# Attention and feed-forward in one block, the integer weights' size check inside attention's groups, Q and K low halves on VectorE

## The reference

```
ga, gb: size clamped to at least 0.25, sign kept
h = layernorm(x) * (1 + ca) + sa
q, k, v = split(h @ W_qkv + b_qkv)                 # 16 heads of 32
q = elu(q / sqrt(32)) + 1.0001 ; k = elu(k) + 1.0001
causal linear attention: kv += k v^T, ks += k, out = (q kv) / (q ks + 1e-6)
x = x + ga * (out @ W_out + b_out)
h = layernorm(x) * (1 + cb) + sb
x = x + gb * ((silu(h @ wg^T) * (h @ wu^T)) @ wd^T)  # wg, wu, wd: int32 / 127, hidden width 1536
```

## Time and profile before

| | us |
|---|---|
| median of 3 runs | 2226.02 (2223.32 to 2226.19) |
| profiled execution, its own time | 2222.91 |
| its span, first to last instruction | 2221.2 |
| TensorE matmul busy | 2144.6 |
| VectorE busy | 1242.6 |
| ScalarE busy | 829.9 |
| GpSimd busy | 846.0 |

### The profile page before, as it was taken

The page is one execution under the profiler, slowest core; times in us unless marked ns, Lnnn a source line. Parts: engine busy times, 40 slices in busy tenths (PEclk is TensorE's granted clock), DMA queues, the critical chain, the costliest instruction groups (busy, mean ns, idle before and its releaser), DMA issues. The chain is left out here.

```text
span 2221.2 us, 38713 instructions
## 1 busy us (share of the span) xinstructions
PE 2144.6 (97%) x15252; PEld 1748.3 (79%) x15252; DVE 1242.6 (56%) x1637; ACT 829.9 (37%) x1383; POOL 846.0 (38%) x634
## 2 busy tenths in 40 slices
PE   5999999999999999999779999999999999999999
PEld 3788887878888787888568888888888888888887
DVE  6988897888888788889732233322233322333211
ACT  4544444444444444444341233322233212332221
POOL 3644544443444444454323233332333323333333
PEclk9999999999999999999889999999999999999999
DMA  6111111111101111111531100111000111001100
GB/s 241 34 54 49 48 40 49 58 49 52 55 30 58 49 54 53 49 53 35 186 133 38 39 10 29 38 38 38 14 28 33 38 38 38 9 28 38 38 20 19
DMA packets 55319, 111.09 MB, mean 50 GB/s; under 512 B 4497, under 2 KB 4497, under 8 KB 55186
## 3 DMA queue, kind: packets, MB, share of 16 engines
q1 hardware_dynamic: 54658, 108.03, 13.9%
q10 hardware_dynamic: 528, 1.05, 0.1%
HBM read 75.50 MB, written 33.56 MB: 49 GB/s over the span
## 5 line engine op out<-in xcount | busy, mean ns | idle before, releaser
L1138 POOL TENSOR_TENSOR h_lo<-h,h_hi 128x512 fp32r<-128x512 f32 x192 | 248.1, 1292 | 498.0 <-ACT h_hi L1208 498.0
L1314 PE MATMUL dn<-wd,h_hi 128*128 128x512 f32 x768 | 298.8, 389 | 0.0
L1314 PE MATMUL dn<-wd,h_lo 128*128 128x512 f32 x768 | 298.8, 389 | 0.0
L1266 DVE TENSOR_TENSOR h<-gu,gate 128x512 f32<-128x512 f32 x192 | 132.4, 690 | 278.2 <-PE gu L1302 242.9
L1208 ACT ACTIVATE h_hi<-h 128x512 fp32r<-128x512 f32 x192 | 121.4, 632 | 386.1 <-DVE h L1266 386.1
L1205 ACT ACTIVATE gate<-gu 128x512 f32<-128x512 f32 x192 | 113.1, 589 | 373.8 <-PE gu L1302 373.8
L1302 PE MATMUL gu<-xt_hi,w_hi 128*128 128x512 f32 x768 | 213.1, 399 | 11.2 <-issue 11.2
L1279 DVE TENSOR_TENSOR fy<-dn,gb_row 128x512 f32<-128x512 f32 x64 | 44.2, 691 | 304.1 <-PE dn L1314 304.1
L656 DVE RECIPROCAL r_den<-r_den 128x512 f32<-128x512 f32 x64 | 213.7, 3339 | 0.0
L1302 PE MATMUL gu<-xt_hi,w_lo 128*128 128x512 f32 x768 | 208.1, 393 | 0.7 <-DVE h L1266 0.2
L1302 PE MATMUL gu<-xt_lo,w_hi 128*128 128x512 f32 x768 | 206.9, 391 | 0.0
(11 more groups left out here) (151 smaller groups left out, 3927.0 us busy)
## 6 DMA issues: line engine op xcount, KB each, us to landing
x_res<-in_L_attn_x SPq DMA_DIRECT2D x64, 256.0 KB, 2.7
x_mid<-x_res SPq DMA_DIRECT2D x64, 256.0 KB, 2.0
fx<-x_mid SPq DMA_DIRECT2D x16, 1024.0 KB, 5.6
out<-fy SPq DMA_DIRECT2D x64, 256.0 KB, 2.0
xg<-in_L_attn_x SPq DMA_DIRECT2D x15, 1024.0 KB, 5.5
fy<-in_L_ffn_w_down SPq DMA_DIRECT2D x12, 256.0 KB, 2.7
xg<-in_L_attn_x ACTq DMA_DIRECT2D x1, 1024.0 KB, 8.5
kt<-in_wmod_t SPq DMA_DIRECT2D x1, 1024.0 KB, 10.3
```

Source lines behind the costliest of these rows:

```text
L1138: pool.tensor_tensor(out=h_lo[:, j, :], in0=h[:, j % 2, :], in1=h_hi[:, j, :].bitcast(F32), op=ALU.subtract).then_inc(h_lo_ready, 1)
L1266: dve.tensor_tensor(out=h[:, j % 2, :], in0=gu[:, 2 * (j % 2) + 1, :], in1=gate[:, j % 2, :], op=ALU.mult).then_inc(h_ready, 1)
L1314: mm = pe.matmul(dn[:, t % 2, :], as_(half[:, j, t * P:(t + 1) * P]), as_(wd[:, j, :]), start=(j == 0 and half is h_hi), stop=(j == HB - 1 ...
```

## The change

There is one block. Each engine runs its attention program and goes on with its feed-forward program; there is no barrier. The feed-forward's tiles are attention's buffers, laid out so that the words land where their floats will stand and are converted in place. The weights come in one array ffn_words of 36 blocks of 128x512 words.

- The size check is spread over the loop's groups 2 to 13: three blocks each are loaded into a buffer `word`, reduced to their largest size, and merged. The comparison is in group 14. TensorE branches there, before the last part of group 14; its usual case is the Then, and holds the rest of attention and the whole feed-forward.
- The words are loaded once more, for conversion: gate and up columns 0 to 1023 in group 14, the rest and w_down in group 15. ScalarE converts them there.
- y shares a_t's buffer, so `divide` also waits for `residual` of the tile before.
- Q's and K's low halves are made by VectorE.
- In group 15 `k_turn` comes before `out_project`; the last tile's `k_turn`, `add_state` and `state_out` are gone. On GpSimd, prod_low of chunk 2 comes after the residual.
- The last out-projection, its gating and residual follow on hidden block 0 of the feed-forward. SyncE's load of groups 0 and 1 of x_mid and of gb come behind attention's last store.

The core of the diff (indentation of moved code is left out of account):

```diff
         @block.tensor
         def _(pe):
+            last_group, last_projection = attn.tensor(pe)
+            pe.wait_ge(att.wide_ready, 1)
+            flag = pe.value_load(wide[0:1, 0:1])
+            with pe.If(flag < 1):
+                last_group()
+                ffn.tensor(pe, True, last_projection)
+            with pe.Else():
+                last_group()
+                ffn.tensor(pe, False, last_projection)
...
-        y = sbuf(s, "y", [P, D])
+    y = a_t
...
+        def load_word(i):
+            wait(sp, most_ready, i + 1)
+            sp.dma_start(word[:, :].bitcast(I32), ffn_words[bass.ds(i, 1), :, :].rearrange("a p n -> (a p) n")).then_inc(word_in, 16)
...
             for t in range(GT):
                 tile = g * GT + t
                 load_residual(tile, t % 2, g * 2 + t // 2)
                 if not isinstance(tile, int) or tile > 0:
                     store(tile - 1, (t + 1) % 2)
+                if not isinstance(g, int) and t < 3:
+                    load_word(g * 3 + (t - 6))
+                if isinstance(g, int) and g == NG - 2 and t == 2:
+                    sp.wait_ge(pj_ready, (NG - 1) * UNITS + 2 * C)
+                    load_wide(words_hi, 0, 0)
+                    load_wide(words_lo, HB, 1)
+                if isinstance(g, int) and g == NG - 1 and t == 0:
+                    sp.wait_ge(pj_ready, NG * UNITS)
+                    load_rest(words_hi, 0, 2)
+                    load_rest(words_lo, HB, 3)
+                    sp.wait_ge(state_ready, (NG - 1) * GT)
+                    for j in range(HB):
+                        sp.dma_start(wd_words[:, j, :], ffn_words[2 * HB + j, :, :]).then_inc(words_in[4 + j // C], 16)
...
         def divide(tile, g, parity, t):
             wait(dve, num_ready, tile + 1)
             wait(dve, rden_ready, (g + 1) * C)
             wait(dve, a_lo_ready, tile)
+            wait(dve, y_ready, tile)
...
+        def word_size(i, slot):
+            wait(dve, word_in, i * 16 + 16)
+            dve.tensor_reduce(most[:, slot:slot + 1], word[:, :].bitcast(I32), AX.X, ALU.max,
+                              apply_absolute_value=True).then_inc(most_ready, 1)
+            wait(dve, most_ready, i + 2)
+            wait(dve, most_merged, i + 1)
+            dve.tensor_tensor(out=most_of_all[:, :], in0=most_of_all[:, :], in1=most[:, slot:slot + 1],
+                              op=ALU.max).then_inc(most_merged, 1)
...
-            for c in range(C):
-                xt_low(0, 0, c)
+        for k in range(C):
+            dve.wait_ge(qk_hi, k + 1)
+            dve.tensor_tensor(out=w_lo[:, k, 0:2 * D], in0=raw_qk[k // 2][:, k % 2, :],
+                              in1=w_hi[:, k, 0:2 * D].bitcast(F32), op=ALU.subtract).then_inc(qk_lo, 1)
+            xt_low(0, 0, k)
...
             divide(g * GT + 3, g, parity, 3)
+            if not isinstance(g, int):
+                word_size(g * 3 + (2 - 6), 2)
...
+        sp.wait_ge(att.a_ready, (NG - 1) * GT)
         load(0, 0)
+        sp.wait_ge(att.xt_ps, (NG + 1) * C)
+        load(1, 1)
+        sp.wait_ge(att.y_gated, NG * GT)
+        sp.dma_start(gb_row[:, :], gb_dram.broadcast_to([P, D])).then_inc(gb_in, 16)
...
                 dve.tensor_tensor(out=h[j % 2], in0=gu[2 * (j % 2) + 1], in1=gate[j % 2],
                                   op=ALU.mult).then_inc(h_ready, 1)
+                if isinstance(g, int) and g == 0 and j == 0:
+                    last_tile()
+                if isinstance(g, int) and g == 0 and j == 1:
+                    clamp_gb()
                 if ahead and j == 0:
                     norm_stats(g + 1, 1 - parity)
...
                     hidden(g, parity, j, wu, 2 * (j % 2) + 1, up_ps)
+                    if isinstance(g, int) and g == 0 and j == 0:
+                        last_projection()
```

More of the change, by code:

```diff
@@ L1 @@
+from collections import namedtuple
 from contextlib import ExitStack
@@ L101, in build @@
[L101 to L114 removed]
+        ga_row = sbuf(top, "ga_row", [P, D])
@@ new lines, in build, with _ @@
+        ffn = feed_forward(nc, top, sem, ident, mod_col, half_neg, w_hi, w_lo, xt_hi, xt_lo, norm, wide, gb_dram, ffn_words,
+                           att, shared, x_mid, out)
+        block = top.enter_context(nc.Block())
+        @block.sync
+        def _(sp):
+            attn.sync(sp)
+            ffn.sync(sp)
+        @block.gpsimd
+        def _(pool):
+            ffn.gpsimd(pool, attn.gpsimd(pool))
+        @block.scalar
+        def _(act):
+            attn.scalar(act)
+            ffn.scalar(act)
@@ new lines, in attention @@
+    z_exp = sbuf(s, "z_exp", [P, 2, GN])
+    z_relu = sbuf(s, "z_relu", [P, 2, GN])
+    kt, qt, v, r_den, probs, prod, prod_hi, prod_lo, k_sum, a_hi, a_lo = turned
+    words_hi, words_lo, wd_words = later.words_hi, later.words_lo, later.wd_words
+    xf = sbuf(s, "xf", [P, 2, GN])
+    k_past = sbuf(s, "k_past", [P, C])
+    kv_diag = sbuf(s, "kv_diag", [P, C, P])
+    k_tok = sbuf(s, "k_tok", [P, D])
+    a_t = sbuf(s, "a_t", [P, D])
+    x_res = sbuf(s, "x_res", [P, 2, D])
+    y = a_t
+    word = sbuf(s, "word", [P, D])
@@ new lines, in attention, with unit_of @@
+    raw_qk = [buf[:, :, :].rearrange("p c n -> p (c n)").rearrange("p (k n) -> p k n", k=2) for buf in (kt[1], qt[1])]
+    raw_v, raw_o = v[1], r_den[1]
+    wt_sa, wt_ca, wt_sb, wt_cb = kt[0], qt[0], v[0], r_den[0]
+    wm_late = (kt[1], qt[1])
+    late_bank = tuple(sc[:, i, :] for i in range(2))
+    c_bc = k_tok[:, :].rearrange("p (k n) -> p k n", k=C)
+    silu_row, junk = a_t, word
+    gb_row, ga_sign = a_t, word
+    def unit_of(u):
+        return (u % 2, u // 2) if u < 2 * C else (2, u - 2 * C)
@@ new lines, in vector, with tensor, x_turn, passes @@
+        groups(dve, 2, NG - 2, group)
+    def tensor(pe, exact, last_projection):
+        def x_turn(g, c):
+            wait(pe, xn_ready, g)
+            wait(pe, xf_ready, (g - 1) * C + c - 1)
+            for t in range(GT):
+                mm = pe.transpose(tp[c % 2][:, t * P:(t + 1) * P], xn[t][:, c * P:(c + 1) * P], ident[:, :])
+            mm.then_inc(xt_ps, 1)
+        def passes(exact):
+            return (lambda ap: ap) if exact else (lambda ap: ap.bitcast(F32))
+        def all_groups(exact):
+            as_ = passes(exact)
+            def hidden(g, parity, j, w, bank, done):
+                for i, (xt, k) in enumerate((xt, k) for xt in (xt_hi, xt_lo) for k in range(C)):
+                    mm = pe.matmul(gu[bank], as_(w[:, k, j * P:(j + 1) * P]), as_(xt[parity][:, k, :]),
+                                   start=(i == 0), stop=(i == 2 * C - 1))
+                mm.then_inc(done, 1)
+            def down(g, t):
+                wait(pe, y_gated, g * GT + t - 1)
+                for j in range(HB):
+                    if t == 0:
+                        wait(pe, h_lo_ready, g * HB + j + 1)
+                        if isinstance(g, int) and g == 0:
+                            pe.wait_ge(att.wd_ready, j + 1)
+                    for half in (h_hi, h_lo):
+                        mm = pe.matmul(dn[t % 2], as_(half[j][:, t * P:(t + 1) * P]), as_(wd[j]),
+                                       start=(j == 0 and half is h_hi), stop=(j == HB - 1 and half is h_lo))
+                mm.then_inc(dn_ps, 1)
+            def group(g, parity):
+                wait(pe, xt_lo_done, g * C)
+                if isinstance(g, int) and g == 0:
+                    pe.wait_ge(att.gu_ready, 4 * C)
+                    if not exact:
+                        pe.wait_ge(w_moved, 16 * 3 * HB)
@@ new lines, in group, with word_blocks @@
+                    if 4 <= j < 8 and (not isinstance(g, int) or g + 1 < NG):
+                        x_turn(g + 1, j - 4)
+                for t in range(GT):
+                    down(g, t)
+            groups(pe, 2, NG - 2, group)
+        all_groups(exact)
+    return Programs(sync, gpsimd, scalar, vector, tensor)
+_INS = ["L0_attn_x", "L0_attn_W_qkv", "L0_attn_b_qkv", "L0_attn_W_out", "L0_attn_b_out",
+        "L0_c", "L0_wmod"]
+_TURNED = ("L0_c",)
+def word_blocks(w_gate, w_up, w_down):
+    wide = [np.asarray(w).T.reshape(C, P, HID // D, D).transpose(0, 2, 1, 3).reshape(HB, P, D) for w in (w_gate, w_up)]
+    return np.concatenate(wide + [np.asarray(w_down).T.reshape(HB, P, D)])
```

2101 lines of the change are left out of this document (1012 added, 1089 removed).

## The result

The changed kernel takes 2216.64 us (median of 8 runs, 2214.95 to 2219.81), the kernel before 2224.53 us (8 runs) beside it: a ratio of 0.9966, 95% interval 0.9955 to 0.9977. It is faster by 7.9 us, where 13.8 were forecast.

What follows compares the result with a forecast made beforehand. TensorE was taken to bound the kernel, busy 2144.6 of 2221.2 us, leaving some 77 us. The terms -4.0 + 4.2 + 2.0 + 0.5 - 25.1 + 8.6 = -13.8 us gave 2212 us, range 2200 to 2222.

Steps and rivals of the forecast that it cites:

- Start, -4.0 forecast: Start: Q and K low halves on VectorE end the first projection near 32.8 instead of 36.8 us, 4.0 us gained.
- Loop, +4.2 forecast: Groups 2 to 13: checks and the later division cost 0.35 us a group behind the last check, 4.2 us lost.
- what is late in tiles 0 to 2 is caught up there: Loop, tile 3: VectorE, idle about 10 us a group, makes up the division's delay of 0.7 to 1.8 us.
- Branch, +2.0 forecast: Group 14: TensorE's branch on the size check, moved from the seam, costs 2.0 us.
- the bound from below: Branch in group 14: nearest from below was a loop's jump back, 4.7 us in 5.
- Conversions, +0.5: Groups 14 and 15: ScalarE's word copies stand ahead of the denominators and may make them late; 0.5 us lost.
- Last group, -25.1 forecast: Last group and seam: no reductions, earlier K turn, x rows' wait; feed-forward's second block at 1111.2, not 1136.38; 25.1 us gained.
- Feed-forward, +8.6 forecast: Feed-forward group 0: group 1's rows load late, TensorE waits 6 us, then half clock 2.6 us; 8.6 us lost.
- (a): Feed-forward: rows of group 1 arrive in time or VectorE is not held; no 8.6 us loss, 2203.6 us; chance 0.17.
- (b): Loop: VectorE-bound at tile 3's V rows, 2.1 us in 12 groups, 25.2 lost instead of 4.2; 2233 us; chance 0.08.
- (c): Last group keeps its pace (4 us), xt_lo always loses (4.2 us): 2220.4 us, no measurable change; chance 0.1.
- (d): Branch costs what it did at the seam, 4.6 us more: 2217 us; chance 0.15.

Runs made afterwards that it cites:

- the two runs: On the changed kernel: twelve unused VectorE reductions put back in the last group, 2223.46 us; last output projection ahead of the first hidden block, 2223.86 us.
- the other arm: The changed kernel with TensorE's condition turned round, so the usual weights take the arm that is jumped to; 2220.19 us, ratio 0.9975.
- xf first on the kernel before: The kernel before, with ScalarE's second xf and xt_hi in the third tile put ahead of a_hi; 2224.57 us, ratio 1.0003.
- no cover: The changed kernel with the last output projection ahead of the feed-forward's first hidden block instead of behind it; 2223.86 us, ratio 0.9997.
- Q, K alone: The kernel before, with only the low halves of the Q and K weights moved from GpSimd to VectorE; 2220.61 us, ratio 0.9989.
- fx first: The changed kernel with the loads of the feed-forward's rows of groups 0 and 1 ahead of attention's last store; 2208.60 us, ratio 0.9934.
- no checks: The changed kernel without the size check's loads, reductions and merges in groups 2 to 13; 2214.30 us, ratio 0.9950.
- the words first: The changed kernel with the last group's 20 word loads ahead of the store of tile 59 instead of behind it; 2211.88 us, ratio 0.9944.

## Why the prediction was right, and where it was not

The direction was right, and so were the causes in three of the four stretches; the loop's was not. The measured 2216.64 us is 4.6 above the forecast, and part of the nearness is luck: in the loop an error of 5.5 us on the bad side stands beside one of 2.5 on the good side. The first paragraph's 77 us are TensorE's idle time alone; matmuls at the lower clock count as busy, so the room was larger.

**Start, -4.0 forecast: right** at its place (-4.76 at 32 us), and for the reasons given: columns at 20.3, ScalarE's own copies, one collision of VectorE with a GpSimd instruction. That VectorE sets the pace up to group 0 was right too. The forecast left out where the halved clock lands, behind the first wait or the second, which is worth 1.6 us, and how long it lasts at the very start, up to 1.1 us. The Trainium skill, SBUF — State Buffer, "Who interferes with whom", made the collision certain; the trace agrees, with 1.77 us instead of 0.69.

**Loop, +4.2 forecast, +9.7 measured: the wrong mechanism.** The step that failed is "what is late in tiles 0 to 2 is caught up there". It was true of VectorE, whose idle time I had counted, and I followed the delayed division no further than to VectorE's own next instructions. Its first consumer is ScalarE's a_hi, and what stands behind a_hi on ScalarE is xf, for which TensorE waits in tile 3. The wait for v that the forecast named as the loop's sign did not grow, it shrank. The forecast named the residual in front of the division and its 0.7 to 1.8 us; the wait is 0.6 us in groups without a check and up to 1.4 with one, where the check has VectorE and so the whole chain later still. The collision of xt_lo and a_lo, on which the 0.35 us a group rested, went the harmless way where I looked (xt_lo at 1000.59, a_lo at 1000.61 with 1.84 us instead of 1.29).

**Branch, +2.0 forecast: 0.** The step that failed is the bound from below: it was a jump, and this is none. The lines of the trace show no gap for the arm ahead and 2.97 us for the other. The Trainium skill, Runtime: NRT & Kernel Launch, "Instruction fetch mechanics", has only a taken branch out of the fetched window wait; these two numbers agree with it. **Conversions, +0.5: 0.** ScalarE waits 5.1 us for words in group 14 and TensorE does not notice. With these two at zero the loop's own error is 5.5 us.

**Last group, -25.1 forecast, -21.0 measured: right mechanism, one term mis-sized.** "The x rows of tile 1 are queued behind the 20 loads" is what happened. The term that was too small is the way of the x rows through the queue. I had the store that precedes the loads 14.0 us behind the scores of tile 60 (13.1 measured), and the rows land 15.8 us behind it; they landed 20.3 us behind it (1081.87 to 1102.2). SyncE took 11.5 us to issue the loads, and the x rows another 8.3 from their issue. That makes 3.6 of the 4.1 us missing. In return the gain has the parts that the forecast gave it: 6.0 us for the reductions and 3.1 to 4.6 for the hidden block in the wait for a_lo are shown by the two runs. The remainder, some 11 us, matches the 11.2 us before the feed-forward's first matmul, which has no counterpart after; no run puts that barrier back alone, and none undoes the earlier turn of K or brings back the last tile's left-out steps, so their shares stay open.

**Feed-forward, +8.6 forecast: +9.0, right**, step by step: issue behind the last store (9.7 us after the last numerators, 9.6 forecast), VectorE at the statistics, 6.9 us of TensorE's idle time (6 forecast), the clock behind it (about 2, where 2.6 were forecast). One run takes 8.9 of it away by queue order alone.

**Rivals.** (a) fell: the wait was there. (b), V rows at their place, fell: that handover gained slack, and even with the wait for xf gone only 0.3 us a group are waited for V rows. (c) had one half right, the last numerators at the old pace (45.8 against 45.6 us), for the x rows' sake and not the residuals' sum, and a loop loss of more than its 4.2. (d) fell, and with the other arm it would be 3.0 us and not 6.6; that its total, 2217, is nearest of all to the measured 2216.6 is luck.

## What to carry to other kernels

When an instruction gets a new wait, follow it through every engine until the chain reaches the engine that bounds: the cost appears at whatever stands *behind* its consumer in that consumer's queue, even if it belongs to other data. A queue's order is free to change, and here three such exchanges, of two copies, of loads and a store, of a store and two loads, were worth over three times the change itself. And test a merged buffer together with the queue orders that were tuned without it.

## What the runs showed of the hardware

- A lower clock can come with a delay and does not follow the length of the wait alone. Behind a wait of 2.33 us the first four matmuls took 1.20 us and the next 1.85; behind one of 2.01 us all kept their pace; with xf first on the kernel before, a wait of 1.97 us left the clock up, and with no cover even one of 3.11 us did (granted clock 1.00 from 1121.85 to 1124.6 us). With Q, K alone one of 1.84 us was followed by four matmuls at 2.03 (granted clock 0.50), and with fx first one of 0.88 us by four at 2.07, when the clock had been low some microseconds before.
- The same stretch of group 0, 83 to 90 us, in windows of TensorE alone (busy, clock, DMA share, GB/s): after it runs at the full clock, in the kernel with no checks, behind a wait of 2.31 us, at 0.76 in the mean, with TensorE busy throughout in both.

```profile
83.00:90.00 7.00, 7.00 (x66) 1.00 0.00 0
```
```profile
83.00:90.00 7.00, 7.00 (x28) 0.76 0.00 0
```

- Which of two neighbouring waits the clock falls behind changes the sum: 1.6 us in group 0 between kernels with the same code there, and up to 2.7 at its end together with how long the low clock lasts at the start. A profile's stretch should be compared with those of several kernels before 2 or 3 us in it are explained.
- Twelve loads of 256 KB each held SyncE's queue for 5.99 us, 0.50 each; four others took 3.62 us in the kernel after and 1.75 with the words first. A residual load, 2.9 us in the median of the page, needed 8.3 from its issue behind them.
